# A fused GroupNorm and lambda-layer block on one core: output tiles moved forward in the loop, two of them from VectorE to GpSimd, another layout for the scattered v and another operand order in 32 matmuls an image

## What is computed

```python
xn = group_norm(x, 32 groups)
h = relu(bn1(conv1x1(xn, conv1_w)))                 # 512 -> 128 channels
q = bnq(conv1x1(h, q_w))                            # 4 heads x 16
k = softmax over 16 of conv1x1(h, k_w)
v = bnv(conv1x1(h, v_w))                            # 32 channels
pos = conv 15 x 15 of every channel of v by emb     # -> 16 x 32 values a pixel
content_lambda = einsum('bkm,bvm->bkv', k, v)
h = einsum('bhkn,bkv->bhvn', q, content_lambda) + einsum('bhkn,bkvn->bhvn', q, pos)
out = x + relu(bn3(conv1x1(relu(bn2(h)), conv3_w)) + xn)
```

## Time and profile before

| | |
|---|---|
| median of 3 runs | 5059.17 us (5052.83 to 5062.59) |
| the profiled execution | 5064.58 us, its span 5062.8 us |
| PE, DVE, ACT, POOL busy | 91%, 60%, 44%, 15% of the span |
| granted TensorE clock, mean | 0.932 of full speed |
| DMA | 1284.17 MB, mean 254 GB/s |
| one pass of the loop (31 in all) | 156.16 us, from 2379.26 to 2535.42 |

### The profile page before, as it was taken

One profiled execution on the slowest core, in us unless ns is written; L12 is line 12 of the kernel. 1 busy time (PEld: TensorE's weight loads), 2 busy tenths in 40 slices (PEclk: granted clock), 3 DMA queues, 4 the chain that ended last, 5 costly groups with the idle time before them and its releaser, 6 DMA issues.

```text
span 5062.8 us, 120727 instructions
## 1 busy us (share of the span) xinstructions
PE 4606.1 (91%) x49366; PEld 2722.9 (54%) x49366; DVE 3032.9 (60%) x4759; ACT 2228.5 (44%) x2752; POOL 744.0 (15%) x433
## 2 busy tenths in 40 slices
PE   4899999999999899999999998999999999999997
PEld 2555555555555555555555555555555555555554
DVE  4466665665655665656656656656566566566564
ACT  1444444444444444444444444444444444444443
POOL 0011110111111111111111111111111111111111
PEclk8899999999999999999999999999999999999998
DMA  3778777788777787777787777887777877778776
GB/s 96 220 258 293 261 233 255 260 267 293 229 248 266 260 289 266 230 254 253 264 295 233 247 261 252 292 269 229 256 253 264 299 239 241 259 256 289 265 228 225
DMA packets 537175, 1284.17 MB, mean 254 GB/s; under 512 B 43049, under 2 KB 225325, under 8 KB 528557
## 3 DMA queue, kind: packets, MB, share of 16 engines
q1 hardware_dynamic: 471276, 1017.22, 62.3%
q10 hardware_dynamic: 65472, 260.05, 14.0%
HBM read 844.79 MB, written 432.33 MB: 252 GB/s over the span
## 4 chain that ended last, share of the span: by engine, by line
PE 73%; DVE 12%; issue 8%; ACT 5%; SPq 1%; DMA 0%; DVEq 0%; ACTq 0%; POOL 0%; POOLq 0%
PE ring L525 18%; PE ring L651 15%; PE ring L506 15%; PE ring L581 10%; PE ring L605 5%; PE ring L532 4%; DVE ring L1028 3%; DVE S L1024 2%; PE ring L537 2%; PE ring L615 2%; ACT region L700 2%; ACT region L791 2%; DVE region L979 1%; DVE region L700 1%; PE ring L515 1%
## 5 line engine op out<-in xcount | busy, mean ns | idle before, releaser
L700 ACT COPY region<-ring 126x1024 f32<-126x1024 f32 x1120 | 1102.6, 1015 | 1129.8 <-PE ring L506 1121.6
L581 PE MATMUL ring<-h,w3T 128*128 128x512 f32 x2048 | 999.1, 631 | 112.4 <-DVE S L1024 79.8
L700 DVE COPY region<-ring 126x1024 f32<-126x1024 f32 x416 | 507.2, 1219 | 694.7 <-PE ring L506 694.7
L506 PE MATMUL ring<-Qt,Ep 96*126 96x256 bf16 x5120 | 831.6, 304 | 96.0 <-ACT region L700 71.2
L525 PE MATMUL ring<-X,w1e 128*128 128x512 f32 x2048 | 908.8, 597 | 3.2 <-DVE w1e L899 3.2
L651 PE MATMUL ring<-region,V 126*32 126x128 f32 x24576 | 865.3, 286 | 20.9 <-issue 20.9
L651 PEld LDWEIGHTS ring<-region,V 126*32 126x32 f32 x24576 | 674.1, 114 | 238.3 <-issue 231.6
L506 PEld LDWEIGHTS ring<-Qt,Ep 96*126 96x126 bf16 x5120 | 616.9, 150 | 327.5 <-issue 156.7
L581 PEld LDWEIGHTS ring<-h,w3T 128*128 128x128 f32 x2048 | 383.1, 198 | 534.9 <-issue 380.0
L525 PEld LDWEIGHTS ring<-X,w1e 128*128 128x128 f32 x2048 | 385.0, 191 | 469.5 <-issue 466.2
L873 DVE BATCH_NORM_STATS2 st<-X 128x6 f32<-128x512 f32 x1024 | 621.5, 678 | 1.7 <-DMA X<-x_dram 1.7
(11 more groups left out here) (127 smaller groups left out, 2974.4 us busy)
## 6 DMA issues: line engine op xcount, KB each, us to landing
X<-x_dram SPq DMA_DIRECT2D x132, 2048.0 KB, 20.3
out_dram<-X SPq DMA_DIRECT2D x512, 512.0 KB, 7.9
X<-x_dram ACTq DMA_DIRECT2D x124, 2048.0 KB, 10.5
Qt<-q_parts SPq DMA_DIRECT2D x768, 128.0 KB, 3.2
V<-v_windows SPq DMA_DIRECT2D x96, 1024.0 KB, 10.2
lambda_sums<-S SPq DMA_DIRECT2D x64, 1024.0 KB, 4.0
h<-lambda_sums SPq DMA_DIRECT2D x256, 256.0 KB, 4.9
q_parts<-region SPq DMA_DIRECT2D x128, 256.0 KB, 3.7
```

Source lines behind the costliest of these rows:

```text
L506: last = nc.tensor.matmul(dst[0:TROWS, i * 256:(i + 1) * 256], taps(u, xo, yo), Q[:, :, xo * BLK + yo, :], start=(i % 2 == 0), stop=True, ...
L581: last = nc.tensor.matmul(dst[:, yb * HALF:(yb + 1) * HALF], w3T[:, t, :], src, start=True, stop=True)
L700: return engine_copy(dst, src)
```

## The change

- Order of the mixed part: `o1.0` now comes before `q2`, `o1.1` before `q3`; `o1.2` and `o1.3` stay behind `k3`. `cp` takes the PSUM buffer of `cl`, so that all later names sit in other buffers.
- Tiles: 10 of 16 on VectorE become 8 (0, 2, 3, 5, 6, 9, 12, 15); GpSimd gets 8. T has four buffers, two of them in h1's place, so the lambda part's first weights wait for the last GpSimd tile.
- `spread_v` writes each row of v to all its places in a layout of 22 columns of 256 values: 8 copies a chunk in place of 3. The store is one DMA with 64 runs of 5376 values, and one for v_rest. vX now lies in the half of `region` that `w0.s` are written to, so these wait for the end of the store (v_out). SP issues the store ahead of the last q loads, and the v loads ahead of the stores of tiles 4 to 15.
- `content` has its operands in another order: the inner run read is 4 neighbouring bf16 values (before: one value, then a step of 16), the inner run written steps by 128 PSUM values (before: neighbours).
- `cl`'s copy goes from VectorE to ScalarE, `cp`'s steps work in PSUM, `softmax_sum` of a chunk runs ahead of the next q, of weights slots 0 VectorE takes 5 and 7 instead of 1 and 5. The zeros of the setup are stored in four DMAs instead of eight.

```diff
-BY_DVE = {0: (1, 5), 1: (1, 3, 5), 2: (1, 3), 3: (3,), 4: (3,), 5: (1, 3, 5, 7)}
+BY_DVE = {0: (5, 7), 1: (1, 3, 5), 2: (1, 3), 3: (3,), 4: (3,), 5: (1, 3, 5, 7)}
...
-VEC_TILES = [0, 2, 3, 5, 7, 8, 10, 12, 13, 15]
+VEC_TILES = [0, 2, 3, 5, 6, 9, 12, 15]
...
+        T = [S[:, 0:2, :].rearrange("p h n -> p (h n)"), S[:, 2:4, :].rearrange("p h n -> p (h n)"), h1[:, 0, :], h1[:, 1, :]]
...
+        vX = region[0:W, PT * DV:PT * DV + WCOLS * ROW].rearrange("p (w r) -> p w r", r=ROW)
+        vXb = vX.rearrange("p w (m v) -> p w m v", v=DV)
...
-                sp.wait_ge(vx_ready, im * (3 * NCH) + 3 * NCH)
-                for a, n in ((0, 8), (8, 8), (16, 5)):
-                    sp.dma_start(vD[PAD:PAD + W, a:a + n, :],
-                                 vX[:, 0:n, a // BLK:a // BLK + NYB, :].rearrange("x r m v -> x r (m v)"))\
-                        .then_inc(v_out, 16)
...
+                sp.wait_ge(vx_ready, im * (8 * NCH) + 8 * NCH)
+                sp.dma_start(vD[PAD:PAD + W, :, :], vX[:, 0:WROWS, :]).then_inc(v_out, 16)
+                sp.dma_start(vR[PAD:PAD + W, :], vX[:, WROWS, :]).then_inc(v_out, 16)
...
-                        nc.tensor.matmul(bank_of(k)[c * DV:(c + 1) * DV, :], CLp[:, :],
-                                         Qg[:, :, c, half * 32:half * 32 + 32, 4 * k:4 * k + 4]
-                                         .rearrange("p h n b -> p b h n"),
+                        nc.tensor.matmul(bank_of(k)[c * DV:(c + 1) * DV, :]
+                                         .rearrange("p (b h n) -> p h n b", b=4, h=HEADS), CLp[:, :],
+                                         Qg[:, :, c, half * 32:half * 32 + 32, 4 * k:4 * k + 4],
                                          start=True, stop=False, skip_group_check=True)
...
+                for k in range(3):
+                    w = BLK * k
+                    a0, a1 = max(2 * j, k - 1), min(2 * j + 2, NYB - 1 + k)
+                    n = 4 if k < 2 else 3
+                    nc.scalar.copy(vXb[:, w:w + 2 * n - 1:2, a0 + 1 - k:a1 + 1 - k, :], odd[:, 0:n, a0:a1, :])\
+                        .then_inc(vx_ready, 1)
+                    nc.scalar.copy(vXb[:, w + 1:w + 6:2, a0 + 1 - k:a1 + 1 - k, :], even[:, 1:4, a0:a1, :])\
+                        .then_inc(vx_ready, 1)
...
             def lead(name, at, im):
+                if name == "w0.0":
+                    act.wait_ge(v_out, im * 32 + 32)
...
+            def keys_out(at, im):
+                act.wait_ge(cl_full, im + 1)
+                nc.scalar.copy(clS, ring[at["cl"]][96:96 + DK, 0:DV]).then_inc(cl_ready, 1)
...
                 if kind == "q":
+                    if j:
+                        softmax_sum(chain, im, j - 1)
...
                 if name == "w0.0":
-                    dve.wait_ge(vx_ready, im * (3 * NCH) + 3 * NCH)
+                    dve.wait_ge(v_out, im * 32 + 32)
```

More of the change, by code:

```diff
@@ L86, in placed @@
             out[name] = 2 + int(name[3:]) % 2
+        elif name == "cp":
+            out[name] = out["cl"]
         else:
@@ L427, in _ @@
             for x0 in (0, PAD + W):
-                for a in range(0, WROWS, BLK):
-                    n = min(BLK, WROWS - a)
-                    sp.dma_start(vD[x0:x0 + PAD, a:a + n, :],
-                                 vX[0:PAD, 0:n, 0:NYB, :].rearrange("x r m v -> x r (m v)")).then_inc(setup_vd, 16)
-                sp.dma_start(vR[x0:x0 + PAD, :], vX[0:PAD, 0, 0:NYB, :].rearrange("x m v -> x (m v)"))\
-                    .then_inc(setup_vd, 16)
-            sp.wait_ge(setup_vd, 8 * 16)
+                sp.dma_start(vD[x0:x0 + PAD, :, :], zeros[:, 0:WROWS, :]).then_inc(setup_vd, 16)
+                sp.dma_start(vR[x0:x0 + PAD, :], zeros[:, WROWS, :]).then_inc(setup_vd, 16)
+            sp.wait_ge(setup_vd, 4 * 16)
             for j in range(NCH):
@@ L462, in _ @@
                 store_q(b + 1, 3)
+                store_v(b + 1)
                 load_q(b + 1, 2)
                 load_q(b + 1, 3)
-                store_v(b + 1)
-                for n in range(4, 8):
-                    store_out(b, n)
                 load_v(b + 1)
-                for n in range(8, 16):
+                for n in range(4, 16):
                     store_out(b, n)
@@ L728, in spread_v @@
                 act.wait_ge(vs_ready, im * NCH + j + 1)
-                a = 2 * j
                 even = vS[0:W, :, :].rearrange("p (a i) v -> p i a v", i=4)
                 odd = vS[W:2 * W, :, :].rearrange("p (a i) v -> p i a v", i=4)
-                nc.scalar.copy(vX[:, 0:8:2, a + 1:a + 3, :], odd[:, :, a:a + 2, :]).then_inc(vx_ready, 1)
-                nc.scalar.copy(vX[:, 1:7:2, a + 1:a + 3, :], even[:, 1:4, a:a + 2, :]).then_inc(vx_ready, 1)
-                nc.scalar.copy(vX[:, 7, a:a + 2, :], even[:, 0, a:a + 2, :]).then_inc(vx_ready, 1)
+                for k in range(3):
[6 more added lines that the diff above has]
+                        .then_inc(vx_ready, 1)
+                    if k < 2:
+                        a0 = max(2 * j, k)
+                        nc.scalar.copy(vXb[:, w + 7, a0 - k:2 * j + 2 - k, :], even[:, 0, a0:2 * j + 2, :])\
+                            .then_inc(vx_ready, 1)
             def relu_half(b, n):
@@ L755, in lam @@
             def lam(b, with_next):
-                act.wait_ge(v_out, b * 64 + 64)
+                act.wait_ge(v_out, b * 32 + 32)
+                act.wait_ge(pool_out, b * NPOOL + HEAD)
                 if with_next:
@@ L813, in _ @@
             sqrt_of_var(0)
[L814 removed]
+            act.wait_ge(setup_vd, 4 * 16)
             for name in PRO:
@@ L927, in lam @@
                 n = 0
-                dve.wait_ge(v_out, b * 64 + 64)
+                dve.wait_ge(v_out, b * 32 + 32)
+                dve.wait_ge(pool_out, b * NPOOL + HEAD)
                 for u in range(UNITS):
```

70 lines of the change are left out of this document (30 added, 40 removed).

## The result

The changed kernel took 5025.5 us (5016.9 to 5028.7) where the kernel before took 5057.2 (5052.8 to 5062.6) in the same runs: a ratio of 0.9934, 95% interval 0.9917 to 0.9951. It is faster by 0.5 to 0.8%, a seventh of what was forecast, and outside the range (4690 to 4960).

A forecast was written before the change was run, and what follows sets the result against it. PE was taken to bound the front and lambda part, VectorE the tail. Tail -3.6 and content -3.9 us a pass, 31 times, with ends -1, gave -234 from 5064.6: 4831 profiled, 4825 as median; range 4690 to 4960.

The forecast's parts named there:

- The bounds of the three stretches: Before the change, PE sets the front (50.74 us) and lambda part (61.46); VectorE sets the tail (43.96) through PSUM buffers.
- The base of the tail: The stretch from k3's last matmul to the first content matmul before the change, taken as 43.96 us a pass.
- The chain by hand, without additions (32.3): Changed tail at full clock: cl at 6.0 us after a 2.4 us wait, first content matmul at 32.3; 8.1 us less.
- Addition 1: Tail, at cl: the 2.4 us wait is followed by slow work, costing about 2 us a pass.
- Addition 2: End of the tail, one weights slot for each move: clock probably 0.50 again, costing 1.5 us a pass.
- Addition 3: Tail, at w0.0, which needs all of q: the loads stand behind the v store, 0 to 4 us, taken as 1.
- The wait for v_out, "covered by 1.4": Tail: moving w0.0 waits for v's store, over by 16.4 us at the latest against 17.8, so covered by 1.4 us.
- Content (-3.9): Content matmuls of the lambda part: groups 0.26 us (full clock) or 0.56 (half) instead of 0.91, saving 3.9 us a pass.
- Ends (-1): First and last image, once each: -2.6 for tiles, -4 for contents, +6 for weights waiting on the v store; about -1 us.
- The stepped writes cost what the reads did: Rival on content's PSUM writes: groups stay at 0.91 us, only the tail's 3.6 is gained, 4947 us; chance 0.18.
- The transfers become the bound: Rival: later output stores delay the next X and the statistics in the lambda part, returning about 3 us a pass, 4918; chance 0.12.
- The chain without the three additions: Rival: tail gains the full 8.1 us a pass and content 3.9 to 5, giving 4670 us; chance 0.2.

The follow-up runs named there:

- e4: The changed kernel with the v path of the kernel before (three copies a chunk, four stores, SP's old order, no v_out wait at w0.0): 4931.1 us.
- e11: The changed kernel with its one store of v cut in three, at the same place ahead of the last q loads: 5077.5 us.
- e1: The changed kernel with both last q loads issued on SP ahead of the v store again: 4967.7 us.
- e3: The kernel before with nothing but the new operand order of the content matmuls: 5012.2 us.
- e6: As e3, but the content matmuls write neighbouring PSUM values instead of stepping by 128; the output is not the reference's: 4964.4 us.
- e7: As e4, with the old split of tiles (ten on VectorE), the old weights slots and the old content order: 4955.2 us.
- e9: As e4, with the old split of tiles and the old weights slots but the new content order: 4931.7 us.
- e10: As e4, with seven eighths of the output of tiles 8 to 15 not stored in the loop: 4838.5 us.

## Why the prediction was wrong, step by step

- **The bounds of the three stretches**: right for the front and the lambda part. That VectorE bounds the tail of the kernel before is what its waits say; with the change it doesn't: 26.8 us busy of 41.2 (forecast near 29), with other waits.
- **The base of the tail**: 43.96 us was one pass; the mean is 42.92. Every gain of the tail was counted from 1.04 us too high, 32 us in all.
- **The chain by hand, without additions (32.3)**: its length is borne out by e4, 33.3 in the pass shown and 33.8 in the mean. Its place for cl is not: with the eight copies it was computed for, cl starts at 6.9 and not 6.0, and waits 3.40 us and not 2.4. The copies took the time forecast; q3's residual on VectorE ended 2.2 us behind k3 and not 1.5, for it stood behind the softmax sums of k2 (until 2415.52), which the change puts ahead of it.
- **Addition 1, slow work behind the wait at cl (2 us)**: about right. In the changed kernel cl and the tile behind it take 2.78 + 2.82 where e4, at clock 1.00, takes 2.04 + 1.98: 1.6 us. In the mean of the passes the clock is at 0.50 for 3.4 us behind cl's start.
- **Addition 2, a slow end of the tail (1.5)**: it is part of e4's 33.8, so about right.
- **Addition 3, the q loads behind the store (1, range 0 to 4)**: this is the step that failed. The wait alone is 3.4 us an image, near the upper end of the 0 to 4 and 2.4 above the 1 that went into the sum, and slow matmuls follow it. I saw that SP's issue would be short (it was, 1.1 us) and took the loads' own 7.61 us as fixed; they took 12.47. The same twelve loads took 12.47, 8.71 (e11) or 7.66 us (e1) to issue, by what was queued ahead of them. e1 shows it: with the loads ahead of the store the tail is 3.2 us shorter. Why SP is held stays open.
- **The wait for v_out, "covered by 1.4"**: costs little in the changed kernel, since Qt is later still, but it appears in e1 (1.30 us in the rows shown). e1's tail is 3.0 us above e4's: PE is idle 1.3 us more of it in the mean, nearly all of that at cl (3.5 an image against 2.3 in e4, for eight copies instead of three), and busy 1.7 us more at the same work, with the clock at 0.50 for 8.7 us of the tail instead of 5.5. v's path in all costs the tail 40.11 - 33.84 = 6.3 us, 4.5 of it idle and 1.8 slower work, where additions 1 and 3 held 3.
- **Content (-3.9)**: the mechanism was right and the size was off. Reads of one bf16 value per 32 bytes held the array at 0.91 us a group, whatever the clock, and the new order frees it; but the group takes 0.44 us at full clock, not 0.26, and 0.86 at half, not 0.56. The saving is (246.0 - 180.7) / 32 = 2.0 us an image. I had named the unknown (stepped writes, priced by 16-column matmuls that "can hide" a penalty) and then gave it no share in the forecast, only a rival that lost all. What came was between the two. The rule on PSUM in the Trainium skill ("PSUM — Partial Sum Buffer", Specifications: non-contiguous patterns slow matmuls significantly) agrees with e3 against e6: stepped writes 0.86 ns a column, neighbours 0.46. The rule on SBUF that I cited from the Trainium skill ("SBUF — State Buffer", Door 1: two or more hits per line) also agrees: one value per 32 bytes took 1.8 ns a column, runs of four with plain writes 0.46. The reads gave the larger part, 246.0 - 106.2 = 140 us of content's busy time, of which the stepped writes took 74.5 back.
- **Ends (-1)**: the start was +5.1 us, as computed (+6), the end 2.9 shorter where 6.6 were added up: +2 in all.

The sum in the profiled execution: tail and front +0.7 a pass where -3.6 was forecast (4.3 missed, 133 us: 32 by the base, 2.4 us a pass or 74 us by addition 3, the other 0.9 by cl's later place and slow clock), the lambda part and content -2.3 where -3.9 was forecast (50 us), the ends 3 us. That is 186 of the 201 us between 4825 and 5026. The rest are the profiled executions themselves, 5 us above the median before and 9 below it now.

**The rivals.** None was the case by itself. "The stepped writes cost what the reads did" (4947) had the right place and twice the price: it took all 3.9 us of content's gain back, and 1.9 were lost. "The transfers become the bound" (4918) isn't what happened in the changed kernel, but every better version has just this wait (e4, e7, e9 and e1), and for e4 e10 shows that it caps. My price for it, 3 us a pass, is e4's against e10's: 62.26 - 59.47 = 2.8. "The chain without the three additions" (4670) needs both a free path of v and a free DMA stretch; e4 has the tail, and e10 without its bytes still takes 4838.

**What follows for the kernel.** New order, old path of v: 4931 us, with or without the split of the tiles. The new path of v is a loss of 93 us here: 63 by the place of the store on SP (e1), the other 30 by what is left of it, the eight copies, the layout with its wait at w0.0 and the place of the v loads, not tried apart. To go on, bytes must leave the stretch around the first content matmul, for the rest of the lambda part has a DMA share of 0.38.

## What to carry to other kernels

Price a DMA that is moved ahead of others by what it does to those behind it, on the queue's own issue as well as at their landing; twelve small loads that were cheap in front of a store were late behind it. When a stretch is shortened, look at the transfers that fill it: a mean DMA share of 0.80 over e4's span hid 55 us at 1.0, and the whole gain of the two moved tiles went there. An operand order has two sides: if a matmul is slow by its reads, price the writes of the new order by a matmul of the same length, or count the unknown in the forecast itself.
